# The drive of a state-space scan made by TensorE from a diagonal matrix instead of by VectorE

## The reference, cut to what matters

```python
def _selective_scan(u, dt, A, Bm, Cm, D):
    dA = jnp.exp(dt[..., None] * A)
    dBu = (dt * u)[..., None] * Bm[:, :, None, :]

    def step(h, inp):
        dA_t, dBu_t = inp
        h = dA_t * h + dBu_t
        return (h, h)
    ...
    y = jnp.einsum('lbdn,bln->bld', hs, Cm)
    return y + u * D
```

## Time and profile before

| | |
|---|---|
| median of 3 runs | 1582.84 us (1582.56 to 1591.12) |
| profiled execution | 1581.95 us, its span 1579.9 us |
| busy PE / DVE / ACT / POOL | 1129.9 / 1216.3 / 701.0 / 433.8 us |
| mean granted TensorE clock | 0.83 of full speed |
| bytes moved by transfers | 74.73 MB |

### The profile page before, as it was taken

One profiled execution on the slowest core, in us unless ns is written; L12 is line 12 of the kernel. 1 busy time (PEld: TensorE's weight loads), 2 busy tenths in 40 slices (PEclk: granted clock), 3 DMA queues, 4 the chain that ended last, 5 costly groups with the idle time before them and its releaser, 6 DMA issues. The chain is left out here.

```text
span 1579.9 us, 14237 instructions
## 1 busy us (share of the span) xinstructions
PE 1129.9 (72%) x4361; PEld 550.6 (35%) x4361; DVE 1216.3 (77%) x1671; ACT 701.0 (44%) x1245; POOL 433.8 (27%) x348
## 2 busy tenths in 40 slices
PE   3885876588767877687766886678777886664654
PEld 1433442244333343333433343234423343321313
DVE  1744679886997699976898779976999769976874
ACT  2532654365433645256432654346452653334221
POOL 2011024510443005420344005430144202431641
PEclk9976988898787889798886998888887987885795
DMA  2000102101220103201121002201021011202210
GB/s 64 1 7 0 48 34 88 53 3 54 67 93 14 56 1 107 67 0 56 43 91 40 22 34 80 83 11 55 20 94 54 1 55 54 100 13 68 94 60 7
DMA packets 31404, 74.73 MB, mean 47 GB/s; under 512 B 4506, under 2 KB 14563, under 8 KB 31331
## 3 DMA queue, kind: packets, MB, share of 16 engines
q1 hardware_dynamic: 31330, 73.83, 14.0%
HBM read 71.20 MB, written 2.62 MB: 47 GB/s over the span
## 5 line engine op out<-in xcount | busy, mean ns | idle before, releaser
L573 POOL TENSOR_TENSOR read<-state,bc_row 128x1024 f32<-128x1024 f32 x128 | 301.7, 2360 | 739.3 <-issue 428.7
L1388 PE MATMUL bank<-read,ident 128*128 128x512 f32 x512 | 318.4, 758 | 169.9 <-POOL read L573 169.8
L1068 DVE TENSOR_TENSOR_SCAN state<-decay,bank 128x1024 f32<-128x1024 f32 x128 | 292.7, 2287 | 16.7 <-ACT decay L657 5.5
L657 ACT ACTIVATE decay<-dt,neg_a 128x510 f32<-128x510 f32 x256 | 169.0, 710 | 235.6 <-DVE state L1068 235.6
L1388 PEld LDWEIGHTS bank<-read,ident 128*128 128x128 f32 x512 | 109.4, 233 | 312.2 <-POOL read L573 207.6
L1325 PE MATMUL bank<-znt,omega 128*128 128x512 f32 x256 | 151.4, 676 | 70.2 <-ACT sqf L648 70.1
L1078 DVE TENSOR_TENSOR s_sb<-bank,causal 128x512 f32<-128x512 f32 x128 | 87.9, 687 | 127.2 <-PE bank L1338 127.2
L1057 DVE TENSOR_TENSOR bank<-dtu,bc_row 128x1024 f32<-128x1024 f32 x128 | 160.7, 1256 | 3.5
L1362 PE MATMUL bank<-s_sb,vext 128*32 128x256 f32 (+1 forms) x1024 | 134.5, 368 | 24.3 <-ACT s_sb L668 24.0
L645 ACT ACTIVATE expf<-bank,minus_s,root2s 128x512 f32<-128x512 f32 x128 | 99.2, 775 | 93.3 <-PE bank L1325 92.9
L668 ACT ACTIVATE s_sb<-bank 128x256 f32<-128x256 f32 x128 | 49.1, 384 | 147.9 <-DVE s_sb L1078 147.9
(11 more groups left out here) (226 smaller groups left out, 1764.2 us busy)
## 6 DMA issues: line engine op xcount, KB each, us to landing
bc_row<-bc_rows SPq DMA_DIRECT2D x128, 512.0 KB, 3.7
xa<-x_dram SPq DMA_DIRECT2D x8, 256.0 KB, 4.0
out_dram<-x SPq DMA_DIRECT2D x8, 256.0 KB, 2.5
omega<-omega_t_dram SPq DMA_DIRECT2D x1, 512.0 KB
bc_rows<-xdbl SPq DMA_DIRECT2D x8, 64.0 KB
wqkv<-w_qkv_t_dram SPq DMA_DIRECT2D x1, 192.0 KB
state<-w_down_dram SPq DMA_DIRECT2D x1, 176.0 KB, 2.4
state<-w_gate_dram SPq DMA_DIRECT2D x1, 128.0 KB, 2.1
```

The lines of the kernel that those rows point to most:

```text
L573: pool.tensor_tensor(read[:, s % STATE_BUFFERS], state[:, s % STATE_BUFFERS], bc_row[:, s % BC_BUFFERS, 1].unsqueeze(1).broadcast_to([P, D ...
L657: last = act.activation(decay[:, s % 2, k, :, 1:], dt[:, k].rearrange("p (b t) -> p b t", b=SEQS)[:, :, 1:], ACT.Exp, scale=neg_a[:, k, s: ...
L1068: dve.tensor_tensor_scan(state[:, s % STATE_BUFFERS].rearrange("p k t -> p (k t)"), decay[:, s % 2].rearrange("p k b t -> p (k b t)"), ban ...
L1388: last = pe.matmul(bank[:, 6 + k], ident[:], read[:, s % STATE_BUFFERS, k], start=(s == 0), stop=(s == STATES - 1))
```

## The change

The drive is no longer made by VectorE. Per group, `dtu` is turned by eight transposes on TensorE into `dtu_t` (tokens on the partitions, copied from banks 4 and 5 by ScalarE), and B by four into `b_t` (one column of 128 tokens per state and tile of tokens). Per state, ScalarE makes four diagonal 128x128 matrices, the identity times a column of `b_t` (`diagonal_in`, two buffers), and TensorE multiplies: drive[channel, token] = sum over tokens' of dtu_t[token', channel] x diagonal[token', token], four matmuls of 128x128 for each half of the channels (`drive`). The scan is done in two halves of one PSUM bank each, and each half of a bank is refilled as soon as its half scan is over. B's rows no longer go through DRAM: only C's 16 rows do, and each row that comes back is 256 KB instead of 512. Scan 0 is done at the end of the turn before, scans 1 to 15 in the first part. GpSimd's read-out of state k waits, instead of for the next drive, for VectorE's `attention_rest` of slot k (`vector_rest`).

```diff
@@ -456,35 +466,34 @@
...
-                    bc_loaded[s % BC_BUFFERS].sem, 16)
+                sp.dma_start(c_dram, xdbl[STATES:BC]).then_inc(c_stored.sem, 16)
+                sp.wait_ge(c_stored.sem, c_stored.at(group, 1))
+
+            def load_c(group, s):
+
+                sp.wait_ge(read_done.sem, read_done.at(group, s + 1 - C_BUFFERS))
+                sp.dma_start(c_row[:, s % C_BUFFERS], c_dram[s].partition_broadcast(P)).then_inc(
+                    c_loaded[s % C_BUFFERS].sem, 16)
...
@@ -563,16 +572,44 @@
...
+            def vector_rest(turn, k):
+
+                new, mid = turn.new, turn.mid
+                if turn.has_new and k == 0:
+                    pool.wait_ge(norm_a.var.sem, norm_a.var.at(new, 1))
+                if turn.has_done and k == 1:
+                    pool.wait_ge(ffn_b.result.sem, ffn_b.result.at(turn.done, 2))
...
+                    pool.wait_ge(ffn_a.result.sem, ffn_a.result.at(mid, 1))
+                if turn.has_mid and k == 14:
+                    pool.wait_ge(norm_b.var.sem, norm_b.var.at(mid, 1))
+
+            def read_out(turn, s):
+
+                group = turn.old
+                loaded_row = c_loaded[s % C_BUFFERS]
                 pool.wait_ge(state_done.sem, state_done.at(group, s + 1))
-
-                pool.wait_ge(drive_done.sem, drive_done.at(group, min(s + 2, STATES)))
+                pool.wait_ge(loaded_row.sem, loaded_row.at(group, s // C_BUFFERS + 1))
+                vector_rest(turn, s)
 
                 pool.wait_ge(y_ps.sem, y_ps.at(group, max(s + 1 - STATE_BUFFERS, 0)))
                 pool.tensor_tensor(
                     read[:, s % STATE_BUFFERS], state[:, s % STATE_BUFFERS],
-                    bc_row[:, s % BC_BUFFERS, 1].unsqueeze(1).broadcast_to([P, DT, TOK]), ALU.mult).then_inc(
+                    c_row[:, s % C_BUFFERS].unsqueeze(1).broadcast_to([P, DT, TOK]), ALU.mult).then_inc(
                         read_done.sem, 1)
 
...
@@ -612,12 +649,10 @@
             def body(turn):
                 for k in range(SLOTS):
                     attention_rest(turn, k)
-                    if turn.has_old and k > 0:
-                        read_out(turn.old, k)
+                    if turn.has_old:
+                        read_out(turn, k)
                 if turn.has_old:
                     deviation(ffn_b.norm, turn.old)
-                if turn.has_mid:
-                    read_out(turn.mid, 0)
                 if turn.is_last:
                     scale_hidden(ffn_b, turn.old, 0)
...
@@ -659,6 +694,15 @@
                         dt[:, k].rearrange("p (b t) -> p b t", b=SEQS)[:, :, 1:], ACT.Exp,
                         scale=neg_a[:, k, s:s + 1])
                 last.then_inc(decay_done.sem, 1)
+
+            def diagonal_in(gb, s):
+
+                act.wait_ge(b_t_done.sem, b_t_done.at(gb, 1))
+                act.wait_ge(drive_ps.sem, drive_ps.at(gb, max(s + 1 - DIAGONALS, 0) * DT))
+                for t in range(TILES):
+                    last = act.activation(diagonal[:, s % DIAGONALS, t], ident[:], ACT.Identity,
+                                          scale=b_t[:, t, s:s + 1])
+                last.then_inc(diagonal_done.sem, 1)
 
             def cross(ga, s):
 
...
                     act.activation(xdbl[:], bank[0:BC + RANK, 7], ACT.Copy).then_inc(
                         xdbl_done.sem, 1)
                 if turn.has_old and k == 7:
                     act.wait_ge(ffn_b.xt_ps.sem, ffn_b.xt_ps.at(old, 1))
                     act.activation(ffn_b.xqt[:], bank[:, 6], ACT.Copy).then_inc(ffn_b.xt.sem, 1)
                 if turn.has_mid and k == 7:
+                    act.wait_ge(b_t_ps.sem, b_t_ps.at(mid, 1))
+                    act.activation(b_t[:].rearrange("p t n -> p (t n)"),
+                                   bank[:, 4, 0:TILES * STATES], ACT.Copy).then_inc(b_t_done.sem, 1)
                     for c in range(DT):
                         act.wait_ge(dt_ps.sem, dt_ps.at(mid, c + 1))
...
@@ -783,6 +830,12 @@
                     ffn_tanh(ffn_b, old, (k - 8) // 2)
                 if turn.has_ffn_b and k == 12:
                     ffn_ht(ffn_b, old, 0)
+                if turn.has_mid and k == 14:
+                    for h in range(DT):
+                        act.wait_ge(dtu_t_ps.sem, dtu_t_ps.at(mid, h + 1))
+                        act.activation(
+                            dtu_t[:, 2 * h:2 * h + 2].rearrange("p t c -> p (t c)"),
+                            bank[:, 4 + h], ACT.Copy).then_inc(dtu_t_done.sem, 1)
 
             def mixer_rest(turn, k):
...
@@ -830,6 +883,8 @@
                     act.wait_ge(dt_exp_done.sem, dt_exp_done.at(mid, 1))
                     act.activation(dt_abs[:], dt_abs[:], ACT.Ln, bias=1.0).then_inc(
                         dt_log_done.sem, 1)
+                if turn.has_mid and k in (10, 11):
+                    diagonal_in(mid, k - 10)
                 if turn.has_mid and k in (13, 14):
                     decay_in(mid, k - 13)
...
@@ -841,6 +896,8 @@
                 for k in range(SLOTS):
                     if turn.has_old and 1 < k + 1 < SLOTS:
                         decay_in(turn.old, k + 1)
+                    if turn.has_old and k + 2 < STATES:
+                        diagonal_in(turn.old, k + 2)
                     attention_rest(turn, k)
                 if turn.has_new:
...
@@ -1049,27 +1106,18 @@
                                                       sqf[:, s % 2], ALU.mult, ALU.mult).then_inc(
                                                           feat_done.sem, 1)
 
-            def drive(gb, s):
-
-                loaded_row = bc_loaded[s % BC_BUFFERS]
-                dve.wait_ge(loaded_row.sem, loaded_row.at(gb, s // BC_BUFFERS + 1))
-                dve.wait_ge(state_done.sem, state_done.at(gb, s))
-                dve.tensor_tensor(
-                    bank[:, DRIVE_BANK:DRIVE_BANK + DT], dtu[:],
-                    bc_row[:, s % BC_BUFFERS, 0].unsqueeze(1).broadcast_to([P, DT, TOK]),
-                    ALU.mult).then_inc(drive_done.sem, 1)
-
             def scan(gb, s):
 
                 dve.wait_ge(decay_done.sem, decay_done.at(gb, s + 1))
-                dve.wait_ge(drive_done.sem, drive_done.at(gb, s + 1))
 
                 dve.wait_ge(read_done.sem, read_done.at(gb, max(s + 1 - STATE_BUFFERS, 0)))
-                dve.tensor_tensor_scan(
-                    state[:, s % STATE_BUFFERS].rearrange("p k t -> p (k t)"),
-                    decay[:, s % 2].rearrange("p k b t -> p (k b t)"),
-                    bank[:, DRIVE_BANK:DRIVE_BANK + DT].rearrange("p k t -> p (k t)"), 0.0,
-                    ALU.mult, ALU.add).then_inc(state_done.sem, 1)
+                for c in range(DT):
+                    dve.wait_ge(drive_ps.sem, drive_ps.at(gb, DT * s + c + 1))
+                    dve.tensor_tensor_scan(
+                        state[:, s % STATE_BUFFERS, c],
+                        decay[:, s % 2, c].rearrange("p b t -> p (b t)"),
+                        bank[:, DRIVE_BANK + c], 0.0, ALU.mult, ALU.add).then_inc(
+                            (half_done if c == 0 else state_done).sem, 1)
 
             def mask(ga, s):
...
@@ -1247,13 +1295,6 @@
                     dve.wait_ge(dt_done.sem, dt_done.at(mid, 1))
                     dve.wait_ge(u_done.sem, u_done.at(mid, DT))
                     dve.tensor_tensor(dtu[:], dt[:], u[:], ALU.mult).then_inc(dtu_done.sem, 1)
-                if turn.has_mid and k == 14:
-                    dve.wait_ge(dtu_done.sem, dtu_done.at(mid, 1))
-                    if turn.has_ffn_b:
-
-                        dve.wait_ge(ffn_b.result.sem, ffn_b.result.at(old, 1))
-                    drive(mid, 0)
-                    scan(mid, 0)
                 if not turn.has_ffn_b:
                     return
...
@@ -1274,13 +1315,11 @@
 
             def body(turn):
                 for k in range(SLOTS):
-                    if turn.has_old and k > 1:
+                    if turn.has_old and k > 0:
                         scan(turn.old, k)
                     if turn.has_mid and k == 0:
                         attention_out(turn.mid, SEQS - 1)
                     attention_rest(turn, k)
-                    if turn.has_old and 1 < k + 1 < SLOTS:
-                        drive(turn.old, k + 1)
                 if turn.has_new:
                     features(turn.new, 0)
...
@@ -1295,8 +1334,7 @@
                     mixer_rest(turn, k)
                 if turn.has_mid:
 
-                    drive(turn.mid, 1)
-                    scan(turn.mid, 1)
+                    scan(turn.mid, 0)
                 if turn.is_last:
                     for pair, f in enumerate((ffn_b, ffn_b_last)):
...
@@ -1373,6 +1411,19 @@
                             bank[:, 3, P * (2 * k + side):P * (2 * k + side + 1)],
                             ctx_t[:, SEQ * side + P * k:SEQ * side + P * (k + 1)], ident[:])
                 last.then_inc(ctx_tok_ps.sem, 1)
+
+            def drive(gb, s):
+
```

(33 more changed lines are left out.)

62 lines of the change are left out of this document (40 added, 22 removed).

## The result

| | median, us | range | profiled span |
|---|---|---|---|
| before | 1583.07 | 1582.56 to 1591.12, 4 runs | 1579.9 |
| changed | 1558.85 | 1558.65 to 1559.36, 4 runs | 1556.8 |

The ratio is 0.9839 [0.9823, 0.9854]: 1.6% faster. The forecast was 1595; the measured time lies in its range, between rival 1 (1579) and rival 3 (1541).

What follows compares the result with a forecast made beforehand. TensorE was to replace VectorE as the scan part's bound. Six full turns at +3.5 us make +21; less 1.5 and 6 in the last two turns, +13.5 on 1581.95 gives 1595 us. Range 1545 to 1625.

Steps and rivals of the forecast that it cites:

- rival 1: TensorE stays at full clock: +0.7 us in each of six full turns, less 7.5, 1579 us; chance 0.2.
- rival 3: A half drive on TensorE costs 0.55 us, like four plain transposes: 5.1 us less a turn, 1541 us; chance 0.2.
- the walk's waits, T(0) to X: Slot-by-slot extra VectorE waits, from scan 0's end (T(0)) to the last drive's old start (X): 18.0 us of 85.8.
- The clock's term: One half-clock stretch of TensorE a turn, at drive 13 behind an idle time, delaying slot 14's down by 2.8 us.
- Slots 1 and 2: VectorE waits 2.2 us more while TensorE finishes the previous group's feed-forward, then both halves of drive 1.
- Half drive: Four drive matmuls for half the channels hold TensorE 1.0 us, so a state costs 2.0 us.
- Basis: The old stretch from scan 1's end to the last drive's start, 81.2 us in the one turn read.
- End of turn: Drives 0 and 1 go and scan 1 moves to the next turn: 4.8 us less, scores 0.4 us late.
- Behind X: After the last drive's old start, 14 us set by GpSimd read-outs and TensorE sums stay; slot 6 later loses 0.5.
- Split: Scanning in two halves costs 0.1 us for each of 14 scans, 1.4 us a turn.
- ScalarE's diagonals: Four 128x128 activations a state take 1.2 us, covered by TensorE; at 1.65 us, 0.3 us more a turn.
- Turns without a new group: The turn without a new group gains 1.5 us and the last turn 6 us.

Runs made afterwards that it cites:

- e8: Changed kernel with extra matmuls of zeros behind the sums of slots 7 (6 of them) and 11 (10), keeping TensorE busy in two gaps; 1558.27 us.
- e3: Changed kernel with every TensorE matmul of the drive issued twice; 1710.24 us.
- e4: Changed kernel with only two of four TensorE matmuls per half drive for states 1 to 15; 1523.37 us.
- e7: Changed kernel with ScalarE's diagonals for states 2 to 15 cut to one activation of eight columns; 1558.38 us.
- e6: Changed kernel with TensorE's sums in slots 6, 10 and 14 put behind its attention and feed-forward pieces; 1516.44 us.
- e9: Changed kernel reordered: hidden transposes and downs one slot earlier, four sums later on TensorE; layer norm rows, hidden copies and decay 14 earlier on ScalarE; 1467.51 us.
- e14: Changed kernel with only the sum of state 12 moved behind the second down in slot 14; 1555.36 us.
- e5: Changed kernel without GpSimd's wait for VectorE's other work of the slot before a read-out (`vector_rest`); 1613.20 us.
- e15: Reordered changed kernel with first features earlier and projections between the sums, plus 20 matmuls of zeros in slot 6 of the second part; 1450.58 us.

## Why the prediction was wrong, step by step

**The step that failed is the walk's waits, T(0) to X.** It put 85.8 us, with the half-clock stretch 88.6, and took a turn of 81.2 to compare with. Measured: 83.1 against a mean of 82.6. A full turn was to get 3.5 us longer and got 5.0 shorter. Of these 8.5 us, 5.5 lie in the walk (88.6 against 83.1), 1.4 in the turn of 81.2, and 1.6 behind X, where a drive was put at nothing. The walk's parts, waits of VectorE beyond those of before:

| slots | predicted | measured |
|---|---|---|
| 1 and 2 | 2.2 | 0.6 |
| 3 | 2.9 | 2.8 |
| 6 and 7 | 3.6 | 3.0 |
| 8 to 11 | 4.3 | 4.0 |
| 14 | 5.0, and 2.8 for the clock | 5.2 |
| sum | 20.8 | 15.6 |

- *The places were right*, all of them: the tanh of the second pair 3.49 (forecast about 4), the second down 4.83 (over 5). The clock's term, 2.8 us a turn, was wrong: the clock did fall (0.61 in 624 to 628 us), but the slower drive lay beside VectorE's own work, and e8 shows the price to be nil. Slots 1 and 2 were put 1.6 too high: the first half of drive 1 came in time.
- *Half drive* 0.89 us back to back, forecast 1.0 from the row of four matmuls. By e3 and e4 the 3.3 us that this makes per turn are worth 0.7 to 2.3. Rival 3 needed it at 0.55; that did not come. The 81 ns per pair that the Trainium skill gives ("TensorE: Matmul & The Clock Gate", section Back-to-back issue gap) are 111 here (1.78 us for 16 records), so the trace does not agree.
- *Basis*: the turn of the earlier trace rows is of the shorter of two kinds that alternate; the mean is 1.4 longer, 8 us over six turns. I had read one turn.
- *End of turn*: -4.5 measured, 4.8 less 0.4 forecast: right.
- *Behind X*: 0.5 more forecast, 1.0 less measured. A group has 16 drives; the prediction took 13 between T and X and two at the end of the turn, and put drive 15, which stood at X, at nothing ("the change leaves them as they are"). VectorE's waits behind X are nearly the same (21.8 us before, 22.1 now); its busy time is 1.2 less, and by instruction that is drive 15. What follows waits for GpSimd, whose first step of the mixer's layer norm lay beside drive 15. That step before and now:

```profile
673.80 1.07 POOL L533 TENSOR_SCALAR b_ln_rstd<-b_ln_mv 128x4 f32<-128x4 f32 x1 [3.21 <-DVE b_ln_mv L917]
```

```profile
666.27 0.19 POOL L542 TENSOR_SCALAR b_ln_rstd<-b_ln_mv 128x4 f32<-128x4 f32 x1 [8.17 <-DVE b_ln_mv L974]
```

  These 0.88 us came back in full: VectorE's first exponential step starts 6.45 us behind X before and 5.57 now.
- *Split*: 1.4 forecast, 0.5 measured (2.32 for a pair against 2.29).
- *ScalarE's diagonals*: 1.26 us, forecast 1.2, covered: right (e7). *Transfers*: nothing: right.
- *Busy times*: VectorE 150 us less (about 140 forecast). TensorE rose by 148, not by more than 200: the drives take 278.0, but the rest runs at a higher clock (0.91 in the mean, 0.83 before), and the sums alone take 61 less (257.0, 318.4 before).
- *Turns without a new group*: 7.5 us faster forecast, 6.6 slower measured. In the first of them VectorE waits 22.1 us of 81.4. In such a turn it has less other work, and waits that a full turn hides come out bare: 4.22 us for a drive, 5.83 for the down. In the last turn VectorE waits 22.1 us too, 5.0 before. Its slots without other work did shrink, to 3.51 from 3.71; the gates, transposes and downs between them took it back:

```profile
1487.15 2.33 DVE L1116 TENSOR_TENSOR_SCAN state<-decay,bank 128x512 f32<-128x512 f32 x2 [1.17 <-PE bank L1423]
...
1490.66 2.33 DVE L1116 TENSOR_TENSOR_SCAN state<-decay,bank 128x512 f32<-128x512 f32 x2 [1.17 <-PE bank L1423]
```

In sum: six turns, each 8.5 us better than forecast, are 51, the last turns 14 worse; that leaves 37 us, and 1595 missed by 36. That the miss was not 51 is luck: two errors of opposite sign. The deeper error is what the waits were taken for. I read "as much TensorE as the part lasts" as a bound by amount, with rivals in TensorE's speed: clock and price of a matmul. e4, e8, e6 and e9 show that its order decides: halving the drive gave 35 us, a clock held in the changed kernel's two gaps none, three moved sums 42, and a reordered list 91. No rival had this.

What stays open: why TensorE falls to half clock at the start of four turns of e14 and one full turn of e6, and not of the changed kernel's, although its idle times just ahead are the same in all of them. The records show what such a stretch costs at each place, not what puts it there.

## What to carry to other kernels

When an engine takes over work from the bound, look through its list again: in this kernel, what the relieved engine waits for had to go ahead of what nobody waits for (sums that only feed an accumulation), and that was worth more than the change itself. Until then read a forecast from each wait, not from busy shares. Judge a half-clock stretch by who waits at its end. Count every instruction that goes away, also where the engine is not the bound. Take the turn that you count from as the mean of several.

## What the runs showed of the hardware

- GpSimd against VectorE, both ways. In e5 one-input steps of 0.53 us take 2.56 beside a read-out. Before the change a small step of the layer norm on GpSimd took 1.15 us while VectorE's two-input drive ran (594.86 to 596.08); after it, with a scan from PSUM beside it, 0.19:

```profile
594.98 1.15 POOL L537 TENSOR_SCALAR a_ln_shift<-a_ln_mv 128x4 f32<-128x4 f32 x1
```

```profile
585.76 0.19 POOL L546 TENSOR_SCALAR a_ln_shift<-a_ln_mv 128x4 f32<-128x4 f32 x1
```

The Trainium skill, "SBUF — State Buffer", section Who interferes with whom, says that a VectorE instruction in its two-port mode, or with two SBUF inputs against a read of GpSimd's, shares a port pair with it, and whoever comes second waits out the whole instruction; these rows agree. By that rule e5 could have been foretold, and the 0.88 us behind X too.
- A float32 matmul of 128x128 takes 0.22 us back to back in the drive (8 in 1.78) and 0.23 in e15 (20 in 4.57).
- Two scans of 128x512 from PSUM take 2.32 us, one of 128x1024 2.29.
